# Four buffers instead of two for the transposed chunks and their differences

## What is computed

```python
q, k, v = (proj_heads(x, w) for w in (Wq, Wk, Wv))
out  = softmax(q @ k.T / 8 + causal_mask) @ v
x    = layernorm(x + out @ Wo.T)
x_prev = concatenate([zeros, x[:, :-1]], axis=1)      # one position earlier
xr = mu_r * x + (1 - mu_r) * x_prev
xk = mu_k * x + (1 - mu_k) * x_prev
r  = sigmoid(xr @ Wr.T)
k_act = square(relu(xk @ Wk.T))
y  = layernorm(x + r * (k_act @ Wv.T))
```

## Time and profile before

| | |
|---|---|
| median of 3 runs | 1341.93 us |
| profiled execution, its own time | 1340.37 us |
| its span on the slowest core | 1339.1 us |
| spans of the 8 cores | 1329.1 to 1339.1 us |
| PE busy | 1228.9 us, 92% |
| ACT busy | 722.9 us, 54% |
| DVE busy | 654.3 us, 49% |
| POOL busy | 340.8 us, 25% |
| mean granted PE clock, core 1 | 0.977 |

### The profile page before, as it was taken

How to read it: one execution, slowest core, us unless ns; L and a number is a source line. 1 busy time by engine, 2 the same in 40 slices (tenths; PEclk the granted TensorE clock), 3 DMA queues, 4 the chain that set the end, 5 groups by cost and what they waited for, 6 DMA issues and landing times.

```text
span 1339.1 us, 46249 instructions; the slowest of 8 cores (1329.1 to 1339.1 us)
## 1 busy us (share of the span) xinstructions
PE 1228.9 (92%) x19268; PEld 612.9 (46%) x19268; DVE 654.3 (49%) x1134; ACT 722.9 (54%) x996; POOL 340.8 (25%) x461
## 2 busy tenths in 40 slices
PE   5988999999989999999889999999998999899776
PEld 2444544444444444446545555444453444344343
DVE  0023456255742536515655466525565255624796
ACT  1344667666656776743513554466755666366121
POOL 4002116311252011422126311531125201431141
PEclk9998999999989999999999999989998999899989
DMA  9996246846413284244654355342551237332312
GB/s 137 206 269 164 90 122 181 164 152 200 142 46 106 77 236 135 80 133 168 212 184 126 126 187 181 112 138 81 166 180 45 81 132 252 113 133 83 127 42 85
DMA packets 55645, 187.40 MB, mean 140 GB/s; under 512 B 11920, under 2 KB 28176, under 8 KB 39952
## 3 DMA queue, kind: packets, MB, share of 16 engines
q0 software_dynamic: 19440, 119.55, 31.2%
q1 hardware_dynamic: 36000, 64.89, 15.3%
HBM read 159.49 MB, written 31.46 MB: 143 GB/s over the span
## 4 chain that ended last, share of the span: by engine, by line
PE 77%; DMA 6%; DVE 5%; issue 4%; ACT 3%; SPq 2%; POOL 2%; DVEq 0%; ACTq 0%; POOLq 0%
PE DB L392 50%; PE S L761 10%; PE PVb L802 10%; PE DEN L825 4%; DMA xr<-wv 3%; ACT P L776 3%; SPq L871 2%; PE S L392 2%; DMA rb<-rec 2%; PE DB L558 1%; DVE rec L863 1%; DMA y<-x 1%; POOL ring L275 1%; DVE x L501 1%; DMA x<-x 0%
## 5 line engine op out<-in xcount | busy, mean ns | idle before, releaser
L776 ACT ACTIVATE P<-S 128x1024 bf16<-128x1024 f32 (+3 forms) x640 | 537.2, 898 | 152.4 <-PE S L761 152.2
L392 PE MATMUL DB<-xT,ring 128*32 128x512 bf16 (+1 forms) x3200 | 216.3, 385 | 19.6 <-DMA xT<-xt 13.3
L761 PE MATMUL S<-QO,Kt 64*128 64x512 bf16 (+3 forms) x1280 | 180.3, 350 | 24.2 <-ACT P L776 22.9
L786 DVE TENSOR_TENSOR P<-P,tri_s 128x512 bf16<-128x512 bf16 x128 | 65.0, 509 | 257.8 <-ACT P L776 257.3
L802 PE MATMUL PVb<-P,Vt 128*32 128x512 bf16 (+3 forms) x2560 | 177.3, 353 | 2.9 <-DVE u_s L320 1.9
L879 POOL TENSOR_TENSOR QO<-u_s,rb 128x512 bf16<-128x512 f32 x63 | 83.4, 1324 | 345.2 <-DMA rb<-rec 270.7
L392 PEld LDWEIGHTS DB<-xT,ring 128*32 128x32 bf16 (+1 forms) x3200 | 108.1, 98 | 97.9 <-issue 30.8
L293 POOL DMA_DIRECT2D ring<-wscr x90 | 51.9, 577 | 386.0 <-PE S L761 211.7
L825 PE MATMUL DEN<-P,ones 128*32 128x256 bf16 (+1 forms) x2244 | 119.6, 268 | 6.0 <-DVE rec L863 5.3
L761 PEld LDWEIGHTS S<-QO,Kt 64*128 64x128 bf16 x1280 | 43.0, 94 | 158.6 <-issue 156.8
L392 PE MATMUL DB<-ring,kact 128*32 128x512 bf16 (+1 forms) x1800 | 112.7, 379 | 2.3 <-issue 2.2
(11 more groups left out here) (127 smaller groups left out, 1268.0 us busy)
## 6 DMA issues: line engine op xcount, KB each, us to landing
ring<-wscr POOLq DMA_DIRECT2D x90, 1024.0 KB, 6.0
rb<-rec SPq DMA_DIRECT2D x504, 32.0 KB, 3.1
x<-x SPq DMA_DIRECT2D x28, 512.0 KB, 6.6
y<-x SPq DMA_DIRECT2D x28, 512.0 KB, 6.6
wscr<-ring SPq DMA_DIRECT2D x12, 1024.0 KB, 7.7
xT<-xt POOLq DMA_DIRECT2D x6, 1024.0 KB, 9.7
ring<-wq POOLq DMA_DIRECT2D x8, 256.0 KB, 21.0
ring<-wk POOLq DMA_DIRECT2D x8, 256.0 KB, 21.3
```

Of the source, the lines that this page charges most:

```text
L392: mi = nc.tensor.matmul(out=b[r:r + w], lhsT=lhs[:, r:r + w], rhs=rhs, start=(cch == 0), stop=(cch == NCH - 1))
L761: mi = nc.tensor.matmul(out=sp[:, 512 * hh:512 * hh + n], lhsT=Kt[r, T * t + 128 * j:T * t + 128 * j + 128], rhs=QO[g % 2][r, SPW * t + q0 ...
L776: tok[("exp", k)] = SE.done(nc.scalar.activation(out=p3[:, :, 0:n], in_=s3, func=AF.Exp, bias=EXP_BIAS, scale=0.125), 0.14 + 2 * n / 1145)
L786: tok[("mask", k0)] = tok[("mask", k0 + 1)] = VE.done(nc.vector.tensor_tensor(out=p4, in0=p4, in1=tri[:].rearrange("p (h w) -> p h w", w=1 ...
```

## The change

Chunk i now goes to buffer `k = i % 4` (NX = 4). Buffers 0 and 1 are the old ones. Buffers 2 and 3 of `x1c` are laid into the memory of the three gate buffers `rbuf` (which become one tensor; columns 0 to 512 and 520 to 1032), and buffers 2 and 3 of `tmp` are the two `krelu` buffers. No memory is added. The waits follow:

- The copy of chunk i waits for `mix` of chunk i-4, and for k of 2 or 3 also for the last three uses of the gate buffers.
- POOL's difference also waits for the last square (POOL's own instruction).
- The relu evacuation of an F item and the tanh of an R item also wait for `mix` of the last two chunks.
- The planner lets a T item start after `mix` of four chunks before.

```diff
+NX = 4
-        rbuf = [sb(f"rbuf{i}", [128, 512], F32) for i in range(NR)]
+        rbuf_f = sb("rbuf", [128, NR * 512], F32)
+        rbuf = [rbuf_f[:, 512 * i:512 * i + 512] for i in range(NR)]
+        x1c += [rbuf_f[:, 520 * i:520 * i + SPW + 1] for i in range(2)]
+        tmp += krelu
...
-                k = i % 2
+                k = i % NX
...
-                                          have(("mix", i - 2)) if i > 1 else None)
+                                          have(("mix", i - NX)) if i >= NX else None,
+                                          *[have(("rfree", r)) for r in range(max(0, rn[0] - NR), rn[0]) if k > 1])
...
-                    GP.need(tc, tok.get(("lastc", g)))
+                    GP.need(tc, tok.get(("lastc", g)), tok.get(("square", fn[0] - 1)))
...
-                                          tok[("square", i - 2)] if i > 1 else None, relu=True)
+                                          tok[("square", i - 2)] if i > 1 else None,
+                                          *[have(("mix", m)) for m in range(tn[0] - 2, tn[0])], relu=True)
...
-                SE.need(t, have(("rfree", n - NR)) if n >= NR else None)
+                SE.need(t, have(("rfree", n - NR)) if n >= NR else None,
+                        *[have(("mix", m)) for m in range(tn[0] - 2, tn[0])])
...
-                return [(0.7, lambda: at(("a", "x", g, 3), *([("mix", tn[0] - 2)] if tn[0] > 1 else []))(),
+                return [(0.7, lambda: at(("a", "x", g, 3), *([("mix", tn[0] - NX)] if tn[0] >= NX else []))(),
```

## The result

The changed kernel takes **0.9852 of the time of the kernel before, 95% interval 0.9806 to 0.9898**: about 19.9 us of 1344.87 less (13.7 to 26.1), at best 1319.54 us in a run. The same kernel, timed again beside three experiments (`after_again`), gave 0.9849 (0.9828 to 0.9870). I had forecast 1326 us, 1.2% less than 1341.93.

A forecast was written before the change was run, and what follows sets the result against it. PE, busy 92% of the span, was taken as the bound, gaining only from fewer waits or higher clock. 6.2 + 6.0 + 4.0 = 16.2 us off 1340.4 gave 1324.2, forecast as 1326; range 1316 to 1338.

The forecast's parts named there:

- the fourth rival: More than forecast: all 19.05 us and some from the other rounds' shuffles, time 1321 to 1316; chance 0.10.
- the three places: Rounds 2, 6 and 5 between transposes and F: PE waits plus low clock of 7.40, 7.26 and 4.39 us, together 19.05.
- The pair of waits: ACT's copies to x1c waiting for DVE's xr, the mix of two chunks before: from 17.9 us to under 3.
- Round 2: Transposes to F: of 7.40 us in copy waits and low clock, 6.2 gained, limited by POOL and softmax.
- Round 5: Chunk 7's copy no longer blocks softmax on ACT: F 2.4 us earlier plus 1.7 for the clock, taken as 4.0.
- The first rival: Three attention units in a row leave small PE waits and the low clock stays: gain 9.5 us, time 1332; chance 0.17.
- two limits: Round 2, before F: POOL's chain gives chunk 7's xk at 384.0, PE with softmax waits arrives at 383.0; gain 6.1 to 6.2.
- chunk 2 at 367.0: Round 2: POOL's subtraction of chunk 2, transposed behind the first V item, can follow chunk 1's, ended 366.1, at about 367.0.
- The second rival: The wait moves to F: POOL at 2.40 us a chunk with a late scaling; gain 4 us, time 1338; chance 0.12.
- The new waits (a) to (d): First F evacuation for xr, copies for the earlier residual, POOL for its last square, tanh for mix: each costs nothing.
- the third rival: Slower: the F evacuation waits for a late xr and holds softmax on ACT; 12 us slower, 1354; chance 0.06.
- The other rounds: Rounds 1, 3, 4 and 7, where the planner shuffles some units: taken as 0, loss bounded at 2 us in all.

The follow-up runs named there:

- e5_rounds_2_6: Four buffers only for the chunks of rounds 2 and 6, two elsewhere; 0.9903 of the kernel before, 13.0 us less.
- e6_round_5: Four buffers only for the chunks of round 5, two elsewhere; 0.9984 of the kernel before, 2.1 us less.
- e10_after_no_columns: The changed kernel without POOL's two small column copies ahead of each subtraction; 0.9880 of the kernel before, against 0.9849 for the changed kernel in that job.
- e1_old_order: Four buffers on the chip, but instruction order and engine choices of the kernel before, the planner reckoning with two; 0.9987 of the kernel before.
- e7_rounds_1_3_4_7: Four buffers only for the transposed chunks of rounds 1, 3, 4 and 7, two in rounds 2, 5 and 6; 0.9955 of the kernel before.

## Why the prediction was right, and where it was off

The time lies inside the range of 1316 to 1338: 1319.54, 1320.58 and 1326.75 us in the runs that the ratio compares, 1326 forecast. The measured change is -1.48%, and its interval holds the forecast -1.2%; the narrower one of `after_again` (-1.30 to -1.72%) just leaves it out. So the forecast was somewhat too small. Two of the three times lie in the band of the fourth rival (1316 to 1321), but the three places did not give the 19.05 us that it was made of; they gave 15.3.

- **The pair of waits** fell from 17.9 us to none, as said (under 3). F started 0.25 us behind the last xk, and the windows ran at 1.00, as said. A stretch at the lower clock in round 3, which I had named as a sign of being wrong, is there (3.4 us from 654.7 on core 4), but it was before as well (3.4 us from 680.2 on that core).
- **Round 2**: 6.2 predicted, 6.2 measured. **Round 6**: 6.0 predicted, 5.4. **Round 5**: 4.0 predicted, 3.7. Sum 16.2 against 15.3; `e5_rounds_2_6` and `e6_round_5` show that each place gives its part alone.
- **The clock**: 2.57 us worked out for round 2 from the slow V items, 2.1 to 2.2 by the table above. Right kind, a little too large. The first rival (the clock falls anyway) didn't come: 1.00 in all three windows, though PE waits 0.30, 0.28 and 0.52 us in the last two units.
- **What limits the gain in round 2.** I had worked out two limits, POOL's chain (384.0) and PE's own work with the softmax (383.0). Counted from the end of chunk 1's subtraction (366.1 there, 361.81 on core 4 of the changed kernel) they are 17.9 and 16.9 us. Measured: the last xk ends after 17.2, PE is free after 17.0, and F starts after 17.4. So both limits were as said to 0.7 us, POOL's came last as said, and `e10_after_no_columns` shows PE's directly behind it:

```profile
378.22 0.75 DVE L584 SCALAR_TENSOR_TENSOR xk<-krelu,muks,rbuf 128x512 bf16<-128x512 f32 x1 [0.99 <-POOL krelu L577]
...
378.48 0.33 PE L832 MATMUL DEN<-P,ones 128*32 128x256 bf16 x4
```

- **The step that failed as a reason: chunk 2 at 367.0.** I let POOL begin chunk 2 0.9 us after the end of chunk 1 and put this down to the free buffers. In the order I had read my rows in, POOL stands there for 4.86 us, with four buffers (`e1_old_order`) still for 4.73; only the new order brings it to 0.94. I had counted the new order as a detail (an attention unit moved by the planner, worth 0.9 us). The sum came out because the change brings this order with it; by the buffers alone it would have been wrong, since they give about 0.1%, within its uncertainty of nothing.
- **The second rival was priced without its trigger.** I said that a late scaling would bring it. In `e1_old_order` the scaling is late (375.68), but POOL had also been idle for 4.73 us before; the wait moved to F to the full 5.12. No run takes the late scaling away by itself, so the shares of the two are not shown.
- **Round 5.** The scaling waited 2.50 us for its transfer before (core 1; 2.07 on core 4) and I left it so. After, POOL took it up behind chunk 5. On core 4 its 0.73 us of idle time ended with a chunk copy by VectorE; on six of the eight cores of `after_again` 0.9 to 1.1 us ended with the transfer, so it still waited, as said, but less. PE's wait of 2.71 us is down to 0.51 and 0.52. The order by itself gives 2.5 of the 3.7 us; the prediction had named both the freed copy and POOL's new order and not told them apart:

```profile
849.46 1.70 POOL L886 TENSOR_TENSOR QO<-u_s,rb 128x512 bf16<-128x512 f32 x1 [0.73 <-DVE rbuf L324]
```

- **The new waits (a) to (d)** cost nothing, as said: no relu evacuation or tanh waits for xr of the mixing line in the changed kernel's list of waits, so the third rival (slower) had no place.
- **The other rounds** are the mis-sized term. I took 0, with a loss of 2 us allowed. The transposes of round 3 give 1.2 us on every core, and `e7_rounds_1_3_4_7` times 6.1 (3.4 to 8.6). The whole change gave 19.9 (13.7 to 26.1), and 20.3 (17.5 to 23.1) in `after_again`. The stretches place 16.5 of it; the other 3 to 4 us lie where one program moves by as much from core to core, and stay unexplained.

## What to carry to other kernels

Buffers and order are one change when a planner reckons with the buffers' waits: run each half alone before putting a gain down to one, because a wait taken off a copy comes back at the consumer unless the producer's chain also starts earlier. When chunks fall behind at a steady pace, count what each further buffer gives (here 3.1 of 6.2 us for the third and the rest for the fourth), and stop when TensorE's own work is as long as the chain; a fifth was not tried. After moving items by hand, look at the in-order queue of the engine that serves another stage: 3.9 us won in front of it were 5.6 us lost behind.

## What the runs showed of the hardware

- VectorE and POOL slow each other in both directions. The prediction had POOL's subtraction at 1.03 and 1.55 us; the mixes go from 0.74 to 1.52 us when subtractions follow without the small copies between. Making POOL faster by 0.83 us a chunk gave 1.9 and 2.5 us in the two places where 4.1 each were expected. The Trainium skill (SBUF — State Buffer, "Who interferes with whom") has a VectorE instruction with two SBUF inputs and a GpSimd one that reads SBUF exclude one another for an instruction's length. The trace agrees in kind: 1.52 is 0.78 more than 0.74, less than one whole subtraction of 1.03.
- The clock fell to 0.50 for 6.8 us within the third of three waits of 1.88, 1.03 and 1.92 us close together, and within a single one of 5.12 and one of 6.56 (in that one at 371.9, where the wait ended at 374.8); in the changed kernel waits of 0.30, 0.28 and 0.52 us in a row didn't lower it. With three buffers, behind a wait of 2.13 us, it was 0.50 for 3.4 us (from 378.5 on core 4).
